# Sums of squares over 128 weight columns at a time in a fused attention and feed-forward kernel

## The reference

```
def _ternary_linear(x, w):
    ...
    rms = jnp.sqrt(jnp.sum(x * x, axis=-1, keepdims=True)) / jnp.sqrt(jnp.asarray(d, x.dtype))
    x_norm = x / (rms + EPS)
    return jnp.einsum('bsd,fd->bsf', x_norm, w_q)
h = jax.nn.gelu(_ternary_linear(x, w_up), approximate=False)
return _ternary_linear(h, w_down)
```

## Time and profile before

| what | value |
|---|---|
| time, median of 3 runs | 274.75 us (273.93 to 276.77) |
| time of the profiled execution | 276.07 us |
| its span | 274.3 us |
| TensorE matmul busy | 230.1 us (84%), 4258 instructions |
| TensorE weight load busy | 205.3 us (75%), 4258 instructions |
| VectorE busy | 187.4 us (68%) |
| ScalarE busy | 165.8 us (60%) |
| GpSimd busy | 96.0 us (35%) |
| mean granted TensorE clock | 0.948 |

### The profile page before, as it was taken

One profiled execution on the slowest core, in us unless ns is written; L12 is line 12 of the kernel. 1 busy time (PEld: TensorE's weight loads), 2 busy tenths in 40 slices (PEclk: granted clock), 3 DMA queues, 4 the chain that ended last, 5 costly groups with the idle time before them and its releaser, 6 DMA issues.

```text
span 274.3 us, 9858 instructions
## 1 busy us (share of the span) xinstructions
PE 230.1 (84%) x4258; PEld 205.3 (75%) x4258; DVE 187.4 (68%) x484; ACT 165.8 (60%) x310; POOL 96.0 (35%) x114
## 2 busy tenths in 40 slices
PE   1798887889999999899988997899889798957730
PEld 1787876779899898789877987798778687947620
DVE  0575588877677874698559755885588776775461
ACT  1474455666666459755975597558953857436640
POOL 6033421412242250635163426342544251161231
PEclk9999999999999999999999999999999989995565
DMA  7733750010010001001100010001000010000001
GB/s 238 203 113 113 231 91 2 4 57 5 2 51 11 22 9 55 1 25 30 32 19 23 24 40 22 23 12 50 22 22 2 2 40 2 6 19 19 0 22 38
DMA packets 18622, 11.67 MB, mean 43 GB/s; under 512 B 2004, under 2 KB 17940, under 8 KB 18452
## 3 DMA queue, kind: packets, MB, share of 16 engines
q1 hardware_dynamic: 17872, 9.94, 12.7%
q10 hardware_dynamic: 708, 1.12, 1.3%
HBM read 8.91 MB, written 2.10 MB: 40 GB/s over the span
## 4 chain that ended last, share of the span: by engine, by line
PE 54%; ACT 15%; issue 13%; DVE 11%; POOL 3%; DMA 2%; POOLq 0%; DVEq 0%; ACTq 0%
PE bank L1006 9%; PE bank L1008 8%; PE bank L1007 7%; PE bank L1151 6%; PE bank L1125 5%; PE bank L1109 3%; ACT Yb L538 3%; DVE CTl L805 3%; ACT CTh L538 2%; ACT L618 2%; ACT gT L618 2%; ACT gTh L538 2%; DMA xq<-in_L_attn_x 2%; PE bank L1215 2%; PE bank L1034 2%
## 5 line engine op out<-in xcount | busy, mean ns | idle before, releaser
L479 POOL TENSOR_TENSOR E<-E,rc 128x400 f32<-128x400 f32 x32 | 27.6, 862 | 116.8 <-DVE rc L827 116.8
L538 ACT ACTIVATE Yb<-bank 128x512 f32<-128x512 f32 x64 | 38.2, 597 | 38.1 <-PE bank L1008 37.5
L805 DVE TENSOR_TENSOR CTl<-bank,CTh 128x512 fp32r<-128x512 f32 x64 | 41.2, 684 | 25.1 <-ACT CTh L538 24.4
L1006 PE MATMUL bank<-xTh,Gh 128*128 128x256 f32 x128 | 39.9, 312 | 7.6 <-ACT Yb L538 6.4
L1006 PE MATMUL bank<-CTh,Mh 128*128 128x256 f32 x128 | 37.3, 291 | 1.6 <-DVE CTl L805 1.4
L1008 PE MATMUL bank<-xTh,Gl 128*128 128x256 f32 x128 | 35.9, 280 | 2.4 <-issue 2.4
L1007 PE MATMUL bank<-CTl,Mh 128*128 128x256 f32 x128 | 36.4, 285 | 1.2 <-issue 1.2
L538 ACT ACTIVATE CTh<-bank 128x512 fp32r<-128x512 f32 x64 | 34.7, 598 | 3.8 <-PE bank L1151 3.5
L1008 PE MATMUL bank<-CTh,Ml 128*128 128x256 f32 x128 | 36.4, 285 | 0.0
L1007 PE MATMUL bank<-xTl,Gh 128*128 128x256 f32 x128 | 35.8, 280 | 0.0
L662 ACT ACTIVATE E<-E 128x400 f32<-128x400 f32 x32 | 17.3, 539 | 29.2 <-DVE E L819 29.0
(11 more groups left out here) (136 smaller groups left out, 484.2 us busy)
## 6 DMA issues: line engine op xcount, KB each, us to landing
raw<-in_L_attn_x SPq DMA_DIRECT2D x36, 64.0 KB
w_sb<-in_L_attn_w_qkv ACTq DMA_DIRECT2D x2, 512.0 KB, 5.7
pt_rows<-PT SPq DMA_DIRECT2D x1, 1024.0 KB, 5.6
R<-pt_rows SPq DMA_DIRECT2D x1, 1024.0 KB, 4.9
xr<-in_L_attn_x SPq DMA_DIRECT2D x6, 128.0 KB
out<-y SPq DMA_DIRECT2D x6, 128.0 KB, 1.8
raw<-in_L_attn_x SPq DMA_DIRECT2D x12, 56.0 KB
xq<-in_L_attn_x SPq DMA_DIRECT2D x2, 256.0 KB, 5.5
```

The lines of the kernel that those rows point to most:

```text
L479: tt(e, e, rc[s % 2][:, :].unsqueeze(2).broadcast_to([P, TILES, WIN]), ALU.mult).then_inc(s_norm, 1)
L538: copy = lambda o, i, **k: nc.scalar.activation(o, i, ACT.Copy, **k)
L805: v.tensor_tensor(ct_view(CTl[s // 4 % 2], s % 4, q), c_view(s, q), ct_view(f32(CTh[s // 4 % 2][:, :, :]), s % 4, q), ALU.subtract).then_i ...
L1006: mm(o, wh, rh, start=start, stop=False, **k)
```

## The change

One function changes. Each product of 32 weight columns, which wrote 32 partitions of the result, gives way to one product of 128 weight columns that writes all 128. For each chunk there were 2 x 4 x 4 = 32 products, and there are 8 now. The result lands in the same places, the semaphores and their counts are the same, and so is the accumulation over the four tiles.

```
                 for i in range(CT):
                     for t in range(FT):
-                        for lo in range(0, P, 32):
-                            ins = mm(ss_bank(n)[lo:lo + 32, CHUNK + i:CHUNK + i + 1],
-                                     squared(n)[:, t, P * i + lo:P * i + lo + 32], ones[:, 0:1],
-                                     start=(t == 0), stop=(t == FT - 1), skip_group_check=True)
+                        ins = mm(ss_bank(n)[:, CHUNK + i:CHUNK + i + 1], squared(n)[:, t, P * i:P * i + P], ones[:, 0:1],
+                                 start=(t == 0), stop=(t == FT - 1), skip_group_check=True)
                 ins.then_inc(f_ss, 1)
```

## The result

The changed kernel takes 281.74 us (median of 4 runs, 280.07 to 283.85) against 275.76 for the kernel before in the same comparison: ratio 1.0228, interval 1.0132 to 1.0324. Its profiled execution took 281.62 us, with a span of 279.4 (before 276.07 and 274.3). Forecast were 279.2 and a range of 274.0 to 283.0.

What follows compares the result with a forecast made beforehand. TensorE's square sums were taken to be on the critical path, with loop waits from running out of instructions. Loop -0.6, chunk 4 +1.0, chunk 5 +2.4, chunks 6 and 7 +1.7: +4.5 on 274.75, 279.2 us; range 274.0 to 283.0.

Steps and rivals of the forecast that it cites:

- The price: Square sums: each 128-column f32 product takes 0.111 us at full clock, 0.214 at half; +0.95 us per loop square sum.
- The rivals with 0.056 and 0.076: Cheaper square-sum products: overlapping loads at 0.056 give 271.7 us (chance 0.10); 0.076 gives no change, 274.4 us (0.13).
- the prediction's own step of 0.024 for 32 columns: Square-sum products: one turn grows by 0.024 us for each 32 more loaded columns, from 0.040 to 0.112 for 128.
- The waits: Loop, after the four square sums: TensorE's waits without releaser, read as running out of instructions, all go, giving back 4.4 us.
- forecast 0.6: Loop, chunks 0 to 3: waits given back, 4.4 us, less longer square sums, 3.8, leave a gain of 0.6 us.
- The cover on VectorE: Loop: VectorE's later sum read moves by 0.5 to 0.6 us but is covered; without cover 2.4 us in all.
- The tail: Chunks 4 to 7 after the loop: longer square sums cost +1.0, +2.4 and +1.7 us, depending on the granted clock.
- chunk 4, forecast +1.0: Tail, chunk 4's square sum at full clock: 1.14 us longer, 0.09 earlier start, everything of chunks 5 and 6 behind it.
- Chunk 5 was forecast at half clock, +2.4: Tail, chunk 5's square sum: 1.03 us becomes 3.43 at half clock, and the +2.4 us goes through to the end.
- the middle of the cases with at least one of them at full clock, +1.7: Tail, chunks 6 and 7: between +0.8 us with both at full clock and +2.5 with chunk 7 at half.
- +5.0: Tail, chunks 6 and 7: cost in us if both square sums and the down products between them run at half clock.
- the last terms of the tail (0.2 and 0.7): Tail, chunks 6 and 7 in the two faster rivals: 0.2 us with product cost 0.056, 0.7 us with 0.076.

Runs made afterwards that it cites:

- e5: Kernel before plus 32 small overwritten products (128 instructions) ahead of TensorE's first transposition, square sums unchanged: 271.8 us.
- e6: Kernel before plus 4 small overwritten products (16 instructions) ahead of TensorE's first transposition; a loss of 6.6 us, profiled executions 286.45 and 284.39 us.
- e1: Kernel before with 128-column products in chunks 0 to 3 only, 32 columns in chunks 4 to 7: 274.79 us against 275.69, ratio 1.0012.
- e2: Kernel before with 128-column products in chunks 4 to 7 only, 32 columns in chunks 0 to 3: 281.58 us, ratio 1.0253.
- e10: Changed kernel (128 columns everywhere) plus the 32 small products of e5 ahead of the first transposition: 281.22 us.

## Why the prediction came out as it did

*The price.* Forecast 0.111 us for a product at full clock and 0.214 at half; measured 0.106 (1.59 us for 15 intervals) and 0.203 to 0.215. From the last transposition to the second product behind, TensorE takes 2.02 us (146.47 to 148.49) instead of 1.06: +0.96, forecast +0.95. The rivals with 0.056 and 0.076 are out. Two readings behind the forecast were a little large, because they took in the end of the last product or the way to the next part: from start to start a pair of 64 columns is 0.058, not 0.064, and four of 32 are 0.034, not 0.040. With these the prediction's own step of 0.024 for 32 columns gives 0.106. The Trainium skill, page "TensorE: Matmul & The Clock Gate", section "LDWEIGHTS (loading the stationary operand)", gives the columns divided by 1.2 in ns, 107 for 128; the full-clock price of this f32 load agrees, and at half clock it measured twice that.

*The waits.* They went, and the reason given for them is shown by e5, e6 and the ends of the packets. The Trainium skill, page "Runtime: NRT & Kernel Launch", section "Instruction fetch mechanics", has the instructions fetched in blocks of 256 and the crossing of a block mostly hidden. The places in the stream agree with the 256; of the fifteen crossings in the loop of the kernel before, eleven are hidden and the four behind a square sum are not. The size of the waits was taken from one profile, 4.4 us; the second shows 3.4. Against the first the loop gained 0.9 us (forecast 0.6), against the second it lost 0.3, and e1's interval says no change. Step by step, chunk 0 lost 0.5 and chunks 1 to 3 gained 0.4 to 0.5, as forecast, with respect to the first profile.

*The cover on VectorE.* The sum is read 3.03 us after the step's first score product instead of 2.45, 0.58 later as forecast; the next scores were not held up: in the list of TensorE's waits those for VectorE are the same as before, row by row, among them one of 1.4 us for `CTl` and one of 1.4 for `AT`.

*The tail.* This is the term that was mis-sized, in its clock. These lines of the kernel before stand against those of the tail above:

```profile
235.16 0.71 PE L1215 MATMUL bank<-ones,gT 128*32 128x1 f32 x64
235.80 0.44 PE L1172 MATMUL bank<-ident,attnS 128*128 128x128 f32 x2
...
254.94 0.58 PE L1189 MATMUL bank<-x1Th,wuT 128*128 128x256 f32 x1 [0.93 <-DVE x1Tl L869]
```

Chunk 4's square sum starts 1.3 us early and the transposition of line 1172 behind it 0.3 early: +1.1 for chunk 4, forecast +1.0. Chunk 5's square sum starts 0.2 early (252.14 against 252.37); in between the two profiles drift apart by up to a microsecond either way, with half clock at other places, and come together again. Chunk 5 was forecast at half clock, +2.4; it met full clock and cost 0.6 (chunk 7's up product at 255.29 instead of 254.94, from 0.2 early to 0.35 late). For chunks 6 and 7 I took the middle of the cases with at least one of them at full clock, +1.7; both met half clock, and they cost 4.7, near the +5.0 that the prediction gives for that case. That the two costs add, because ScalarE has one buffer for the squares and VectorE's slack is 1.25 us, held. The profiles of e2 and e10, with the same tail, have chunk 5 at full clock and chunks 6 and 7 at half as well. But chunk 5 also met full clock in the second profile of the kernel before: the +2.4 rested on where the clock happened to fall in the first. Why the clock falls where it does stays open.

The errors are 1.8 us too much for chunk 5 and 3.0 too little for chunks 6 and 7. They cancel in part, which is luck: the spans differ by 5.1 us, and the forecast was 4.5. In the sums of the two faster rivals the last terms of the tail (0.2 and 0.7) don't follow from the steps shown; by those of the main sum they would be nothing and about 0.5, which changes neither rival's place.

*The other side.* The median rose by 6.0 us against 4.5; the interval of the ratio, 3.6 to 8.9 us, holds both.

## What to carry to other kernels

In these runs an f32 product with one moving column costs its weight load (0.034 us for four loads of 32 columns side by side, 0.058 for two of 64, 0.106 for one of 128), so narrow loads side by side were the cheap form, and fewer instructions bought only the end of a wait. Where a profile shows TensorE idle without a releaser, count its instructions and see when the last packet of the instruction queue ended: here some 130 loads and 130 products in 2 us emptied the stream at a fixed place modulo 256. Moving the square sum away from the scores gave 0.9 per cent, and 128 more instructions ahead of everything 1.1. Squares in bf16 (eight products in 0.20 us) do away with both costs, at the price of slightly less exact sums: 0.9836 of the time before.

## What the runs showed of the hardware

The wait for instructions stands at a place of the stream, not at a product, and its length varies between executions of one program (0.25 or 0.36 us lost at chunk 0, 0.9 or 1.5 at chunk 1). What hardly varies is its end: 1.25 to 1.57 us after the packet of 16 KB has left the queue, in twenty waits of five profiles. What does vary is the packet: at these waits it starts 0.3 to 1.6 us after the instructions of the packet before begin to run, and takes 0.9 to 1.4 us. What happens between the end of the packet and TensorE's next product these traces don't show.

Sixteen loads of 128 columns, one after the other without a gap, did not bring the granted clock up: both square sums that began at 0.50 in the changed kernel ended there, while TensorE's records show it busy throughout. And an idle stretch of 1.1 to 2.1 us inside the 64 narrow products was followed by half clock after seven of the eight square sums in the two profiles of e6's kernel (the eighth, of 1.22 us, was not), where waits of 1.35 us and less behind the square sum never were in the kernel before. Why the one and not the other, these runs don't tell.
